# A table of expert units behind every image, and 28 expert chunks hosted inside the image steps

## The chip, the cores and the metric

The kernel runs on one core of a Trainium2 chip. The metric is the time of one execution on the device, in microseconds (us). The cores' engines work side by side, each on its own queue in order, and meet only at semaphores: TensorE (PE) multiplies, VectorE (DVE) and ScalarE (ACT) do the elementwise work and the reductions, GpSimd (POOL) issues the indirect transfers and one addition, SyncE (SP) issues the plain transfers.

## The reference

32 images of 224x224 are cut into 1024 patches each and pass through one attention block and one block of eight experts. Cut to what matters:

```python
h = patches @ W.T + b + pos                      # 32 images, 1024 tokens, 64 wide
q, k, v = h @ Wq.T + bq, h @ Wk.T + bk, h @ Wv.T + bv
prob = softmax(q @ k.T / 8)                      # 1024 x 1024 for each image
h = layernorm(h + (prob @ v) @ Wo.T + bo)
x = h.reshape(32 * 1024, 64)
idx = argmax(softmax(x @ gate_w + gate_b))       # one expert of 8 for each token
pos = cumsum(one_hot(idx)) at idx - 1            # the token's place in its expert
kept = pos < C                                   # C = ceil(1.25 * 32768 / 8) = 5120
y = relu(x @ w1[idx] + b1[idx]) @ w2[idx] + b2[idx]
h = layernorm(h + nan_to_num(y * prb * kept))
```

A token's expert and its place are known only when its own image and all before it have been through attention and gate.

## The kernel before

**Two kinds of work.** Attention goes image by image. The experts' part goes by *chunks* of 4 units; a *unit* is 256 rows of one expert, so that one weight set serves it. There are `NC` = 34 chunks. The gate gives every token a slot in the region of its expert in a table in HBM (`slots`), and POOL scatters an image's 1024 rows there (`scatter`, 8 indirect transfers). A chunk is loaded from `slots` by SP (`load_chunk`: rows into `b_in`, weights into `b_w`), goes through two matmul layers (`rows_turn`, `up`, `down`, `turn_back`) and a last layernorm on DVE and ACT, and POOL scatters its 1024 finished rows to the output (`spread_out`, 8 indirect transfers, 6 for the last chunk).

**Steps.** The program is written out in steps b = -2 to 33 (`run_windows`). In step b the scores, exponents and weighted sums of image b run, beside the row maxima of image b+1, the projection of b+2, the tail of image b-1 (`attend`, the residual, layernorm, gate) and the slots of image b-2 (`positions` on PE, `slot_read` and `slot_index` on DVE, `scatter` on POOL). Each engine's order within a step is fixed by hand: a loop over k or j = 0 to 7, one for each block of 128 keys or queries, with the other work hung in between.

**Chunks inside steps.** `HOST` says which steps host a chunk: chunk c runs in step `HOST[c]`, its last part on DVE in the two steps behind, and its `spread_out` two steps behind. Before, these are the steps 6 to 32, so chunks 0 to 26 (`INSIDE` = 27). The seven others run behind the last step, in `rounds` on every engine. In `rounds` the POOL queue holds nothing but `spread_out`; ahead of chunk `LAST` = 29, the first with rows of image 31, it waits until every earlier output transfer has landed.

**Tables.** Which unit a chunk takes is not known ahead. DVE writes it into `tab` by some dozen small instructions, each waiting for the one before: `count_rows` (1 instruction, in `slot_read`), `full_units` (4), `past_experts` (2), `name_units` (3), and afterwards `take_units` (3), which marks those units as taken. `IMAGE[c]` is the image behind whose slots the units of chunk c are named; an image in `TABLES` gets such a table, and PE then makes two more small matmuls in `positions`. Before, `TABLES` holds the even images 2 to 28, and 30 and 31: a table of an even image names 8 units, for the chunks of two steps.

**Where the table work stands on DVE.** In a normal step b, with image b-2 in `TABLES`: `take_units(b - 3)` and `full_units(b - 2)` at j = 1 ahead of `attend(b - 1)`, `past_experts` at j = 2 ahead of `weigh`, `name_units` at j = 3. Before, the last three stand in even steps, `take_units` in odd ones. Steps 31 and 32 are different (`late_step`): there is no row maximum left to do, the residual is added on DVE instead of POOL (`last_residual`), and on ACT `norm_root` comes right after exponent 2 of the step, ahead of exponent 3. Between `last_residual(30)` and `sum_squares(30)` DVE has `take_units(28)`.

**SP.** `load_chunk` for the chunk of step b+1 stands at the end of step b. It waits for `tab`, for the scatters of image `IMAGE[c]`, and its four weight loads wait for scores of step b.

Of the kernel before, what the change touches and what calls it, by code (L numbers as in the profile page):

```python
# [16 lines left out]
NB = 32  # L17
# [40 lines left out]
PACK = 1 << 19  # L58
NC = (NB * S // UNIT + E) // 4

HOST = [*range(6, NB + 1)]
INSIDE = len(HOST)


def image_of(c):

    if c < INSIDE:
        return (HOST[c] - 3) // 2 * 2
    for n in (NB - 4, NB - 2):
        if c < n - 1:  # L70
            return n
    return NB - 1


IMAGE = [image_of(c) for c in range(NC)]
# [12 lines left out]
def build(nc, x, posT, wqk, wide, deep, w, out):  # L88
    slots = nc.dram_tensor("slots", (SLOTS, ROW), F32, kind="Internal").ap()
    with ExitStack() as ctx:  # L90
# [141 lines left out]
        def per_token(ap, n):  # L232

            return ap.unsqueeze(2).broadcast_to([P, NT, n])

        def per_column_e(ap, n):

            return ap.unsqueeze(1).broadcast_to([P, n, E])
# [20 lines left out]
        def back_place(c):  # L259

            return p_misc[:, 1, :] if c < INSIDE and HOST[c] < NB else p_st[:, 1, :]

# [91 lines left out]
        def chunk_of(b):  # L354

            return HOST.index(b) if b in HOST else None

# [29 lines left out]
        def _(sp):  # L387
# [20 lines left out]
            def load_chunk(c):  # L408
# [21 lines left out]
                def weights_in():  # L430
                    if c >= NBUF:
                        sp.wait_ge(b_yT_ready, c - NBUF + 1)
                    for k in range(2 * PAIRS):
                        v, u = k // 2, k % 2
                        if c < INSIDE:

                            sp.wait_ge(st_done, NT * (HOST[c] - 1) + NT // 2 + 1 + k)
                        sp.dma_start(b_w[:, r, v, u, :], w[bass.ds(e[k], 1), :, :].rearrange("a k f -> (a k) f"))\
# [55 lines left out]
        def _(pe):  # L494
# [125 lines left out]
            def rows_turn(c):  # L620
# [4 lines left out]
                if c < INSIDE:  # L625
                    pe.wait_ge(t_ready, min(HOST[c], NB))
                elif c == INSIDE:
# [329 lines left out]
        def _(dve):  # L957
# [83 lines left out]
            def attend(n, p):  # L1041

                def step(i, ins):
                    ins.then_inc(tail_v, 1)
                    dve.wait_ge(tail_v, TS * n + i)

                dve.wait_ge(turn_done, n + 1)
                dve.wait_ge(v_ready, 2 * n + 2)
                after(dve, uc_ready, n)
                step(1, dve.reciprocal(rs[:, :].rearrange("p (a t) -> p a t", a=2), turned[:, :, :, GT - 1]))  # L1050
                step(2, dve.scalar_tensor_tensor(out=mk[:, :], in0=hh[:, p, :, GH - 1], scalar=0.0,
                                                 in1=rs[:, :], op0=ALU.not_equal, op1=ALU.mult))
                step(3, dve.scalar_tensor_tensor(out=rm[:, :], in0=hh[:, p, :, GH - 2], scalar=0.0,
                                                 in1=mk[:, :], op0=ALU.not_equal, op1=ALU.mult))
                dve.tensor_tensor(four(tt[:, :, :]), turned[:, :, :, 0:CG],  # L1055
                                  four(per_token(rm[:, :], CG)), ALU.mult).then_inc(t_ready, 1)

            def last_residual(n):

                dve.wait_ge(t_ready, n + 1)  # L1060
                dve.wait_ge(rows_ready, n)
                dve.wait_ge(sq_ready, n)
                dve.tensor_tensor(uc[:, :, :], tt[:, :, :], hh[:, n % 2, :, 0:CG], ALU.add)\
                    .then_inc(uc_ready, 1)
# [12 lines left out]
            def sum_squares(n):  # L1077
                dve.wait_ge(sq_ready, n + 1)
                after(dve, rstd_ready, n)
                dve.tensor_reduce(vs[:, :], sq[:, :, :], AX.X, ALU.add).then_inc(vs_ready, 1)  # L1080
# [40 lines left out]
            def table(ins):  # L1121

                steps[0] += 1
                ins.then_inc(table_step, 1)
                dve.wait_ge(table_step, steps[0])
# [5 lines left out]
            def full_units(n):  # L1131


                last = n == TABLES[-1]
                if last:
                    table(dve.tensor_scalar(t_up[:, :], t_cnt[:, :], float(UNIT - 1), None, ALU.add))
                ends = t_up if last else t_cnt
                table(dve.tensor_scalar(t_f[:, :], ends[:, :], -UNIT, None, ALU.bitwise_and))
                table(dve.tensor_tensor(t_av[:, :], t_f[:, :], c_next[:, 0:E], ALU.subtract))
                if last:  # L1140
                    table(dve.tensor_tensor(t_s[:, 0:E], t_cnt[:, :], t_av[:, :], ALU.subtract))
                table(dve.tensor_tensor(t_cum[:, :, :], per_column_e(t_av[:, :], E),
                                        c_tri[:, :].rearrange("p (a b) -> p a b", b=E), ALU.mult))
                table(dve.tensor_reduce(t_c[:, 1:E + 1], t_cum[:, :, :], AX.X, ALU.add))

            def past_experts(n):

                k = TAKEN[TABLES.index(n)]
                table(dve.tensor_tensor(t_ge[:, 0:k, :], c_unit[:, 0:k].unsqueeze(2).broadcast_to([P, k, E]),
                                        per_column_e(t_c[:, 1:E + 1], k), ALU.is_ge))  # L1150
                begin, end = (t_s, t_cnt) if n == TABLES[-1] else (c_next, t_f)
                table(dve.tensor_tensor(t_da[:, :], begin[:, 1:E + 1], end[:, :], ALU.subtract))

            def name_units(n):


                i = TABLES.index(n)
                k, at = TAKEN[i], STARTS[i]
                table(dve.scalar_tensor_tensor(out=t_rd[:, 0:k, :], in0=per_column_e(t_da[:, :], k), scalar=float(PACK),
                                               in1=t_ge[:, 0:k, :], op0=ALU.add, op1=ALU.mult))  # L1160
                table(dve.tensor_reduce(t_r[:, 0:k], t_rd[:, 0:k, :], AX.X, ALU.add))
                dve.scalar_tensor_tensor(out=tab[:, at:at + k], in0=t_r[:, 0:k], scalar=c_next[:, 0:1],
                                         in1=c_unit[:, 0:k], op0=ALU.add, op1=ALU.add).then_inc(table_ready, 1)
# [15 lines left out]
            def take_units(n):  # L1179

                rows_taken = float(UNIT * TAKEN[TABLES.index(n)])
                table(dve.tensor_scalar(t_m[:, :], t_c[:, :], rows_taken, None, ALU.min))
                table(dve.tensor_tensor(t_x[:, :], t_m[:, 1:E + 1], t_m[:, 0:E], ALU.subtract))
                table(dve.tensor_tensor(c_next[:, 0:E], c_next[:, 0:E], t_x[:, :], ALU.add))
# [23 lines left out]
            def weigh(c):  # L1208
                r = c % NBUF
                dve.wait_ge(b_back_done, c + 1)  # L1210
                if c >= 1:
                    dve.wait_ge(b_num_ready, c)
                dve.tensor_tensor(b_p[:, :, :].rearrange("p (u j) d -> p u j d", u=2), turned_back(c),
                                  b_in[:, r, :, :, D].unsqueeze(3).broadcast_to([P, 2, CT, D]), ALU.mult)\
                    .then_inc(b_p_ready, 1)

            def finite(c):

                dve.wait_ge(b_p_ready, c + 1)
                dve.tensor_scalar(b_fin[:, :, :], b_p[:, :, :], 0.0, 0.0, ALU.mult, ALU.is_equal)  # L1220
                dve.tensor_scalar(b_pos[:, :, :], b_p[:, :, :], 0.0, 1e4, ALU.max, ALU.min)
# [27 lines left out]
            def sum_of_squares(c):  # L1249
                dve.wait_ge(b_sq_ready, c + 1)  # L1250
                if c >= 1:
                    dve.wait_ge(b_sd_ready, c)
                dve.tensor_reduce(b_vs[:, :], b_sq[:, :, :], AX.X, ALU.add).then_inc(b_vs_ready, 1)

            def scaled(c):
                dve.wait_ge(b_rs_ready, c + 1)
                if c >= NOUT:
                    dve.wait_ge(b_scattered[c % NOUT], 16 * NT * (c // NOUT))
                dve.tensor_tensor(b_o[:, c % NOUT, :, :], b_c[:, :, :], per_token(b_rs[:, :], D), ALU.mult)\
                    .then_inc(b_o_ready, 1)  # L1260

            def late_step(n, q, back, done):

                last = n == NB - 1
                sum_of_squares(done)
                attend(n, q)
                last_residual(n)
                if not last:
                    take_units(n - 2)
                scaled(done)  # L1270
                sum_squares(n)
                weigh(back)
                gate_logits(n)
                gate_gaps(n)
                gate_choice(n)
                norm_rows(n)
                finite(back)
                slot_read(n)
                probability(n, q)
                slot_index(n, q)  # L1280
                to_numbers(back)
                residual_sum(back)
                centre(back)
                full_units(n)
                past_experts(n)
                if last:
                    name_last(n)
                else:
                    name_units(n)
                    take_units(n)  # L1290
# [224 lines left out]
```

## Time and profile before

| | us |
|---|---|
| median of 3 runs (1049.13 to 1049.90) | 1049.55 |
| the profiled execution | 1052.52 |
| its span, the time that the rows cover | 1050.7 |
| PE busy in the span | 945.6 (90%) |
| DVE busy | 854.0 (81%) |
| ACT busy | 708.1 (67%) |
| POOL busy | 586.2 (56%) |
| granted TensorE clock, mean share | 0.953 |

The profiled execution took 1.8 us more than its span, and 3.0 us more than the median of the unprofiled runs. In the page's 40 slices PE is at nine tenths or more from slice 3 to slice 34 and falls off in the last five; POOL is busiest there.

### The profile page before, as it was taken

How to read it: one execution, taken by the hardware profiler on the slowest of the kernel's cores; microseconds unless marked ns; L12 is line 12 of the kernel's file. 1: busy time of each engine (PE TensorE's matmuls, PEld its weight loads, DVE VectorE, ACT ScalarE, POOL GpSimd, SP SyncE). 2: the span in 40 equal slices, each digit the busy share in tenths (PEclk: the TensorE clock that was granted, in tenths of full speed). 3: DMA queues.
4: the chain of work that ended last, by engine and by line, in shares of the span. 5: the costliest groups of instructions: out<-in, count | busy, mean ns of one | idle time of the engine just before them, and what ended most of it. 6: DMA issues, size and time to landing. Idle time of an engine off the chain costs nothing.

```text
span 1050.7 us, 19710 instructions
## 1 busy us (share of the span) xinstructions
PE 945.6 (90%) x6046; PEld 530.5 (50%) x6046; DVE 854.0 (81%) x1771; ACT 708.1 (67%) x1254; POOL 586.2 (56%) x564
## 2 busy tenths in 40 slices
PE   4799999999999999999999999999999999846640
PEld 2355555555555555555555555555555555433320
DVE  3667788789898989999898989898999988675561
ACT  2365665777777777777777777777777766636650
POOL 0003333335666666666666666666666666776775
PEclk9699999999999999999999999999999999958775
DMA  3322223333434343343434333434333432235200
GB/s 96 80 64 68 59 60 100 99 92 88 117 83 119 96 106 93 98 107 103 110 95 109 105 103 84 118 89 113 102 99 91 108 96 71 87 86 175 63 20 11
DMA packets 72504, 96.25 MB, mean 92 GB/s; under 512 B 15923, under 2 KB 52230, under 8 KB 72398
## 3 DMA queue, kind: packets, MB, share of 16 engines
q1 hardware_dynamic: 55566, 77.87, 28.9%
q0 software_dynamic: 16832, 17.11, 5.1%
q8 instruction: 49, 0.80, 0.3%
q14 instruction: 57, 0.47, 0.1%
HBM read 43.68 MB, written 18.11 MB: 59 GB/s over the span
## 4 chain that ended last, share of the span: by engine, by line
PE 51%; DVE 29%; issue 9%; ACT 8%; DMA 1%; POOL 1%; SPq 0%; POOLq 0%; ACTq 0%; DVEq 0%
PE p_u L601 14%; PE p_st L579 9%; DVE mx L1028 8%; PE p_misc L616 6%; PE p_misc L547 4%; PE p_misc L664 3%; ACT uu L807 3%; PE p_sm L561 3%; PE p_st L583 3%; DVE lo L1020 2%; DVE qk L1013 2%; PE p_misc L524 2%; PE p_sm L680 2%; ACT b_h L852 2%; PE p_misc L680 1%
## 5 line engine op out<-in xcount | busy, mean ns | idle before, releaser
L1399 POOL DMA_INDIRECT slots<-rows,idx x256 | 251.2, 981 | 275.5 <-issue 166.9
L1412 POOL DMA_INDIRECT out<-b_o,b_ix x270 | 294.7, 1091 | 86.7 <-issue 81.7
L1028 DVE TENSOR_REDUCE mx<-p_sm 128x1 f32<-128x1024 f32 x252 | 306.9, 1218 | 35.1 <-PE p_sm L563 33.7
L802 ACT ACTIVATE pT<-p_st 128x1024 f32<-128x1024 f32 x256 | 262.0, 1023 | 92.2 <-PE p_st L585 80.8
L601 PE MATMUL p_u<-pT,vv 128*64 128x512 f32 x1024 | 254.1, 607 | 0.0
L579 PE MATMUL p_st<-hi,hx 64*128 64x512 f32 x256 | 127.4, 498 | 6.2 <-ACT pT L802 4.4
L581 PE MATMUL p_st<-hx,hi 64*128 64x512 f32 x256 | 127.4, 498 | 0.0
L601 PEld LDWEIGHTS p_u<-pT,vv 128*64 128x64 f32 x1024 | 61.8, 136 | 106.2 <-issue 94.4
L579 PEld LDWEIGHTS p_st<-hi,hx 64*128 64x128 f32 x256 | 47.0, 184 | 128.5 <-issue 100.3
L561 PE MATMUL p_sm<-kh,hi 64*128 64x512 f32 x252 | 100.7, 399 | 5.1 <-DMA hx<-hi 3.5
L852 ACT ACTIVATE b_h<-p_misc,b_w 128x256 f32<-128x256 f32 x244 | 95.8, 476 | 13.1 <-PE p_misc L664 6.5
L579 PE MATMUL p_st<-lo,hx 64*128 64x512 f32 x256 | 100.8, 394 | 0.0
L581 PE MATMUL p_st<-lx,hi 64*128 64x512 f32 x256 | 100.7, 394 | 0.0
L585 PE MATMUL p_st<-hx,lo 64*128 64x512 f32 x256 | 100.5, 393 | 0.0
L583 PE MATMUL p_st<-hi,lx 64*128 64x512 f32 x256 | 100.5, 393 | 0.0
L563 PE MATMUL p_sm<-kh,hx 64*128 64x512 f32 x252 | 100.5, 399 | 0.0
L1390 POOL TENSOR_TENSOR uc<-tt,hh 128x576 f32<-128x576 f32 x30 | 39.3, 1312 | 80.3 <-DVE tt L1055 80.3
L773 ACT ACTIVATE qk<-p_misc 128x1024 f32<-128x1024 f32 x32 | 32.9, 1027 | 72.7 <-PE p_misc L524 71.4
L547 PE MATMUL p_misc<-w_px,xt 114*128 114x137 f32 x504 | 76.7, 296 | 0.0
L547 PEld LDWEIGHTS p_misc<-w_px,xt 114*128 114x128 f32 x504 | 63.7, 192 | 23.1 <-issue 23.1
L664 PE MATMUL p_misc<-b_xT,b_w 64*128 64x256 f32 x488 | 68.6, 400 | 4.3 <-ACT b_xT L841 2.5
L616 PE MATMUL p_misc<-w_j,uu 128*128 128x73 f32 x512 | 64.2, 279 | 7.6 <-ACT uu L807 7.0
(189 smaller groups left out, 1818.7 us busy)
## 6 DMA issues: line engine op xcount, KB each, us to landing
b_w<-in_w SPq DMA_DIRECT2D x136, 193.5 KB
hx<-hi SPq DMA_DIRECT2D x64, 256.0 KB, 3.6
b_in<-slots SPq DMA_DIRECT2D x136, 66.0 KB
lx<-lo SPq DMA_DIRECT2D x32, 256.0 KB, 3.1
xt<-in_x SPq DMA_DIRECT2D x32, 196.0 KB
out<-b_o,b_ix POOLq DMA_INDIRECT x270
kh<-kh SPq DMA_DIRECT2D x32, 128.0 KB, 2.3
lx<-lo SPq DMA_DIRECT2D x32, 128.0 KB, 3.0
```

The costliest lines, as they stand in the source:

```text
L547: last = pe.matmul(projected(n, r)[:, j // 2, (j % 2) * GP:(j % 2 + 1) * GP], xt[0:KTOK, n % 3, t * P:(t + 1) * P], w_px[:, :], start=True ...
L561: pe.matmul(max_place(n, j)[:, 0, :], hi[t][0:D, j * P:(j + 1) * P], kh[n % 2][0:D, 0:HALF], start=True, stop=True)
L579: pe.matmul(p_st[:, 0, :], hx[t][0:D, kt], upper[t][0:D, 0:HALF], start=first, stop=False, skip_group_check=k > 0)
L581: pe.matmul(p_st[:, 1, :], hi[t][D:P, kt], lower[t][D:P, HALF:S], start=first, stop=False, skip_group_check=k > 0)
L583: pe.matmul(p_st[:, 0, :], lx[t][0:D, kt], hi[t][0:D, 0:HALF], start=False, stop=k > 0, skip_group_check=k > 0)
L601: last = pe.matmul(p_u[c:c + D, a, :], vv[:, p, NT - 1 - k, :], pT[k % 4][:, a * HALF:(a + 1) * HALF], start=(r == 0), stop=(r == 3))
L616: last = pe.matmul(p_misc[:, j // 4, (j % 4) * GT:(j % 4 + 1) * GT], uu[:, j * P:(j + 1) * P], w_j[:, :], start=True, stop=True)
L802: act.activation(pT[k % 4][:, :], flat(p_st), ACT.Exp).then_inc(exp_done, 1)
L852: act.activation(b_h[:, f, u, v, :], place[:, u, v * UNIT:(v + 1) * UNIT], ACT.Relu, bias=b_w[:, r, v, u, W1C + HB * D + f:W1C + HB * D + ...
L1028: dve.tensor_reduce(mx[:, p, at:at + 1], flat(max_place(n, j)), AX.X, ALU.max).then_inc(max_done, 1)
L1399: pool.indirect_dma_start(slots, bass.IndirectOffsetOnAxis(ap=idx[:, p, j:j + 1], axis=0), rows[:, p, j, :], None, bounds_check=SLOTS - 1, ...
L1412: pool.indirect_dma_start(out_rows, bass.IndirectOffsetOnAxis(ap=b_ix[:, o, j:j + 1], axis=0), b_o[:, o, j, :], None, bounds_check=T - 1, ...
```

## The change

`HOST` begins at step 5 instead of 6: 28 chunks run inside steps and six behind them. `image_of` names the units of the chunk in step b behind image b-3, for every b. `TABLES` becomes the images 2 to 31, 30 tables instead of 16, each of the first 28 with 4 units. Where an even step had 10 table instructions on DVE and an odd step 3, every step from 5 on has 13; altogether 14 tables of 13 instructions more. `late_step(30)` gets the table of image 29 in four new lines.

```diff
--- before.py
+++ after.py
@@ -58,18 +58,15 @@
 PACK = 1 << 19
 NC = (NB * S // UNIT + E) // 4
 
-HOST = [*range(6, NB + 1)]
+HOST = [*range(5, NB + 1)]
 INSIDE = len(HOST)
 
 
 def image_of(c):
 
     if c < INSIDE:
-        return (HOST[c] - 3) // 2 * 2
-    for n in (NB - 4, NB - 2):
-        if c < n - 1:
-            return n
-    return NB - 1
+        return HOST[c] - 3
+    return NB - 2 if c < NB - 3 else NB - 1
 
 
 IMAGE = [image_of(c) for c in range(NC)]
@@ -1267,6 +1264,10 @@
                 last_residual(n)
                 if not last:
                     take_units(n - 2)
+                    full_units(n - 1)
+                    past_experts(n - 1)
+                    name_units(n - 1)
+                    take_units(n - 1)
                 scaled(done)
                 sum_squares(n)
                 weigh(back)
```

`NC`, `LAST`, the buffers and the work of a chunk are the same. Line numbers in the changed kernel are 3 lower than before up to `late_step`, and 1 higher behind it.

**DVE in step 31**, between the last residual (`uc`) and the sum of squares (`vs`) of image 30. `t_m`, `t_x` and `c_wide` are `take_units`, `t_f` to `t_c` `full_units`, `t_ge` and `t_da` `past_experts`, `t_rd` to `tab` `name_units`; `b_o` is the end of a hosted chunk. Before:

```order
L1063 TENSOR_TENSOR uc<-tt,hh 128x576
L1182 TENSOR_SCALAR t_m<-t_c 128x9
L1183 TENSOR_TENSOR t_x<-t_m 128x8
L1184 TENSOR_TENSOR c_wide<-c_wide,t_x 128x8
L1259 TENSOR_TENSOR b_o<-b_c,b_rs 128x512
L1080 TENSOR_REDUCE vs<-sq 128x8
```

Changed, the last 12 of the 17 rows from `uc` to `vs` (ahead of these stand `uc`, the same three `take_units` rows, `t_f` and `t_av`):

```order
L1139 TENSOR_TENSOR t_cum<-t_av,c_wide 128x64
L1141 TENSOR_REDUCE t_c<-t_cum 128x8
L1146 TENSOR_TENSOR t_ge<-c_wide,t_c 128x32
L1149 TENSOR_TENSOR t_da<-c_wide,t_f 128x8
L1156 SCALAR_TENSOR_TENSOR t_rd<-t_da,t_ge 128x32
L1158 TENSOR_REDUCE t_r<-t_rd 128x4
L1159 SCALAR_TENSOR_TENSOR tab<-t_r,c_wide 128x4
L1179 TENSOR_SCALAR t_m<-t_c 128x9
L1180 TENSOR_TENSOR t_x<-t_m 128x8
L1181 TENSOR_TENSOR c_wide<-c_wide,t_x 128x8
L1256 TENSOR_TENSOR b_o<-b_c,b_rs 128x512
L1077 TENSOR_REDUCE vs<-sq 128x8
```

Twelve small instructions have come in between `uc` and `vs`.

**DVE in step 11**, an odd step that hosts a chunk, from the row maximum (`mx`) of j = 1 on; `rs` to `tt` are `attend`, `b_p` is `weigh`. Before:

```order
L1028 TENSOR_REDUCE mx<-p_sm 128x1
L1182 TENSOR_SCALAR t_m<-t_c 128x9
L1183 TENSOR_TENSOR t_x<-t_m 128x8
L1184 TENSOR_TENSOR c_wide<-c_wide,t_x 128x8
L1050 RECIPROCAL rs<-p_misc 128x8
L1051 SCALAR_TENSOR_TENSOR mk<-hh,rs 128x8
L1053 SCALAR_TENSOR_TENSOR rm<-hh,mk 128x8
L1055 TENSOR_TENSOR tt<-p_misc,rm 128x576
L1028 TENSOR_REDUCE mx<-p_sm 128x1
L1213 TENSOR_TENSOR b_p<-p_misc,b_in 128x512
L1259 TENSOR_TENSOR b_o<-b_c,b_rs 128x512
```

Changed:

```order
L1025 TENSOR_REDUCE mx<-p_sm 128x1
L1179 TENSOR_SCALAR t_m<-t_c 128x9
L1180 TENSOR_TENSOR t_x<-t_m 128x8
L1181 TENSOR_TENSOR c_wide<-c_wide,t_x 128x8
L1135 TENSOR_SCALAR t_f<-t_cnt 128x8
L1136 TENSOR_TENSOR t_av<-t_f,c_wide 128x8
L1139 TENSOR_TENSOR t_cum<-t_av,c_wide 128x64
L1141 TENSOR_REDUCE t_c<-t_cum 128x8
L1047 RECIPROCAL rs<-p_misc 128x8
L1048 SCALAR_TENSOR_TENSOR mk<-hh,rs 128x8
L1050 SCALAR_TENSOR_TENSOR rm<-hh,mk 128x8
L1052 TENSOR_TENSOR tt<-p_misc,rm 128x576
```

Four rows of a table (`t_f` to `t_c`) stand ahead of `attend`; behind the next `mx` come `t_ge` and `t_da` ahead of `b_p`, and three more behind the `mx` after that. An even step gets the three rows `t_m` to `c_wide` instead.

**POOL from step 31 to the end**: `slots` are the scatters of the images 29, 30 and 31, `out` the finished rows of chunks. Before:

```order
L1399 DMA slots<-rows,idx 264448x66 x8
L1412 DMA out<-b_o,b_ix 32768x64 x8
L1399 DMA slots<-rows,idx 264448x66 x8
L1412 DMA out<-b_o,b_ix 32768x64 x8
L1399 DMA slots<-rows,idx 264448x66 x8
L1412 DMA out<-b_o,b_ix 32768x64 x70
```

Changed:

```order
L1400 DMA slots<-rows,idx 264448x66 x8
L1413 DMA out<-b_o,b_ix 32768x64 x8
L1400 DMA slots<-rows,idx 264448x66 x8
L1413 DMA out<-b_o,b_ix 32768x64 x8
L1400 DMA slots<-rows,idx 264448x66 x8
L1413 DMA out<-b_o,b_ix 32768x64 x62
```

Behind the last scatter stand 62 output transfers instead of 70, those of one chunk fewer.

## Rows read from the trace of the kernel before

**Rows 1.** Page: the chain of work that ended last, shares by engine.
```profile
PE 51%; DVE 29%; issue 9%; ACT 8%; DMA 1%; POOL 1%; SPq 0%; POOLq 0%; ACTq 0%; DVEq 0%
```

**Rows 2.** Timeline, PE: start, length, then the transpose that opens steps 5, 6, 10, 11, 12.
```profile
158.82 0.33 PE L568 MATMUL p_sm<-c_wide,mx 128*128 128x128 f32 x1
182.67 0.33 PE L568 MATMUL p_sm<-c_wide,mx 128*128 128x128 f32 x1
...
295.43 0.33 PE L568 MATMUL p_sm<-c_wide,mx 128*128 128x128 f32 x1
323.70 0.33 PE L568 MATMUL p_sm<-c_wide,mx 128*128 128x128 f32 x1
351.92 0.33 PE L568 MATMUL p_sm<-c_wide,mx 128*128 128x128 f32 x1
```

**Rows 3.** Timeline, DVE in step 10: its only idle times (in brackets, with releaser).
```profile
304.57 0.21 DVE L1050 RECIPROCAL rs<-p_misc 128x8 f32<-128x8 f32 x1 [0.28 <-PE p_misc L616]
...
308.58 0.69 DVE L1213 TENSOR_TENSOR b_p<-p_misc,b_in 128x512 f32<-128x512 f32 x1 [0.86 <-PE p_misc L641]
```

**Rows 4.** Timeline, DVE: a comparison of step 4's table; below, POOL's addition.
```profile
146.47 1.77 DVE L1149 TENSOR_TENSOR t_ge<-c_wide,t_c 128x32 f32<-128x32 f32 x1
...
146.84 1.34 POOL L1390 TENSOR_TENSOR uc<-tt,hh 128x576 f32<-128x576 f32 x1
```

**Rows 5.** Timeline, DVE in step 31: `take_units(28)`, then table 30 from first to last.
```profile
897.39 0.26 DVE L1182 TENSOR_SCALAR t_m<-t_c 128x9 f32<-128x9 f32 x1
...
897.88 0.17 DVE L1184 TENSOR_TENSOR c_wide<-c_wide,t_x 128x8 f32<-128x8 f32 x1
898.08 0.69 DVE L1259 TENSOR_TENSOR b_o<-b_c,b_rs 128x512 f32<-128x512 f32 x1
...
909.88 0.17 DVE L1138 TENSOR_SCALAR t_f<-t_cnt 128x8 uint32<-128x8 uint32 x1
...
912.31 0.17 DVE L1184 TENSOR_TENSOR c_wide<-c_wide,t_x 128x8 f32<-128x8 f32 x1
```

**Rows 6.** Timeline, ACT and PE in step 31: who waits for `vs`, and on.
```profile
899.40 0.30 ACT L819 ACTIVATE sd<-vs,b_eps 128x8 f32<-128x8 f32 x1 [1.28 <-DVE vs L1080]
...
901.40 0.50 PE L579 MATMUL p_st<-hi,hx 64*128 64x512 f32 x1 [1.54 <-ACT pT L802]
```

**Rows 7.** Stretches: length, busy PE, PEld, DVE, ACT, POOL, clock, DMA share, GB/s.
```profile
900.70:904.10 3.40, 2.70 (x30) 1.82 (x30) 2.90 (x12) 2.49 (x6) 2.79 (x3) 1.00 0.21 54
...
917.70:921.10 3.40, 1.82 (x17) 1.70 (x17) 2.06 (x6) 0.05 (x1) 2.66 (x3) 1.00 0.34 112
921.10:934.70 13.60, 8.87 (x48) 4.81 (x46) 9.36 (x30) 4.91 (x13) 10.56 (x11) 0.50 0.40 116
...
951.90:955.20 3.30, 3.30 (x16) 1.52 (x14) 0.00 (x0) 0.27 (x1) 2.69 (x3) 0.50 0.88 254
```

**Rows 8.** Timeline, PE: the 16 matmuls of one `down` at either clock.
```profile
910.35 1.95 PE L680 MATMUL p_misc<-b_h,b_w 128*64 128x256 f32 x16
...
951.74 3.60 PE L680 MATMUL p_sm<-b_h,b_w 128*64 128x256 f32 x16 [0.78 <-ACT b_h L852]
```

**Rows 9.** Timeline, POOL behind the steps: first transfer of chunks 27, 28, 29; the last.
```profile
969.10 1.11 POOL L1412 DMA_INDIRECT out<-b_o,b_ix  x1 [2.89 <-DVE b_o L1259]
...
979.94 1.48 POOL L1412 DMA_INDIRECT out<-b_o,b_ix  x1 [0.30 <-issue]
...
992.63 1.19 POOL L1412 DMA_INDIRECT out<-b_o,b_ix  x1 [2.12 <-issue]
...
1042.39 0.97 POOL L1412 DMA_INDIRECT out<-b_o,b_ix  x1 [0.30 <-issue]
```

**Rows 10.** Timeline, SP loads chunk 29's rows; ACT copies chunk 28's; page: time to landing.
```profile
946.59 2.07 SPq L428 DMA_DIRECT2D b_in<-slots  x4
...
949.61 0.61 ACT L834 ACTIVATE b_x<-b_in 128x512 f32<-128x512 f32 x1
...
kh<-kh SPq DMA_DIRECT2D x32, 128.0 KB, 2.3
```

## The prediction

> **What bounds the kernel now.** I read the shares of the chain that ended last first [rows 1]: PE carries 51% and DVE 29%, so the kernel is bound by PE with DVE close behind, and a change that loads DVE to relieve the end has to be costed at both. Next I read the step length off PE's own timeline, from the transpose that opens each step [rows 2]. Step 5, the last without a chunk, took 182.67 - 158.82 = 23.85 us. In the steady state, with a chunk, an even step (10) took 28.27 and an odd one (11) 28.22, although DVE has 10 table instructions in the one and 3 in the other. Then the idle times of DVE inside step 10 [rows 3]: 0.28 us before `rs` and 0.86 before `b_p`, both waits for PE, 1.14 us together and no others. DVE is nearly full there, but PE sets the pace. Last I read the two places where this is not so. In step 31 ACT stands 1.28 us until DVE's `vs` is there, and PE stands 1.54 until ACT's exponent [rows 6], so the path runs through DVE. Behind the steps POOL has one idle time of 2.89 us, where it waits for the finished rows of chunk 27, and one of 2.12 ahead of chunk 29; from there to the start of its last transfer, 49.76 us later, it issues without a stop [rows 9]. That end is POOL's, and its beginning hangs on the compute chain of the first chunk behind the steps.
>
> **The change, part by part.**
>
> *One chunk fewer behind the steps.* Between POOL's wait for the first chunk behind and its wait ahead of chunk 29 there were two chunks (27, 28), now there is one (28). The removed one is 979.94 - 969.10 = **10.8 us** [rows 9]. Both waits stay, and chunk 29 and its followers are what they were. So the gain is 10.8 us only if the first chunk's rows are ready no later than now, measured from the end of the steps.
>
> *Step 5 hosts a chunk.* It goes from 23.85 to the length of a hosting step with a table, 28.27: **+4.4 us**. The end of that chunk falls into steps 6 and 7, which then hold what the steady steps hold.
>
> *Thirteen table instructions in every step.* An even step gets `take_units`, three instructions. From `t_m` to `c_wide` and the next start they take 898.08 - 897.39 = 0.69 us [rows 5]. The first 0.28 of it falls into the wait before `rs`, the rest moves `attend` by 0.4 and is taken up by the 0.86 before `b_p` [rows 3], behind which nothing has changed. I take 0, since 0.69 is less than 1.14. The cover is the two waits for PE; without it the price would be up to 0.4 us a step. An odd step becomes what an even one is, which costs the measured difference, 28.27 - 28.22 = 0.05 us, in 12 steps (7 to 29): **+0.6 us**. This includes the two small matmuls of `positions` on PE.
>
> *POOL's addition beside the tables.* In step 4 `t_ge` took 1.77 us, where it lay over POOL's addition of 1.34 [rows 4]. [...] The steady steps with a table already include whatever `t_ge` loses to that addition, and they are 0.05 longer than those without; both start behind `tt`, so they move together. I take nothing beyond the 0.05. Steps 5 to 7 may show one or two long ones (0 to 1 us).
>
> *The table of image 29 in step 31.* It comes between `uc` and `vs` of image 30, 12 instructions in a row, each waiting for the last. The same 12 for image 30 took from 909.88 to 912.31, and the last of a `take_units` holds the next for 0.20 (897.88 to 898.08): 2.43 + 0.20 = **2.6 us** [rows 5]. Nothing hides them. ACT already waits for `vs`, and behind `norm_root` in its queue stand exponent 3 and all exponents after it; PE's scores 4 wait for exponent 3 [rows 6]. So PE's wait grows from 1.54 to 4.2 us. Later in the step DVE has slack, and the rest moves along with PE.
>
> *TensorE's clock in step 31.* [...] The price is bounded by 0 (the low clock lies inside the wait) and by several stretches. The shortest, 951.90 to 955.20, cost 3.60 - 1.95 = 1.65 us on the 16 matmuls of `down` [rows 8]. I take one such stretch: **+1.6 us**; the upper bound is two, +3.3. [...]
>
> *Loads.* SP's wait for the scatter of image b-2 was there in even steps, which load for odd ones, and now is in odd steps too. Behind it in the queue stand only the weight loads, which wait for the end of the step, and the next step's transfers. I take 0. At the end, chunk 29 is the second behind the steps instead of the third. Its rows were issued until 946.59 + 2.07 = 948.66; the nearest landing time is 2.3 us for a 64 to 128 KB transfer, which gives 951.0, and ACT wanted the rows of the chunk in that place at 949.61 [rows 10]. That would be 1.4 us late at most. POOL's scatters move less than the compute chain (POOL does not run through step 31's wait), so part of it is made good: bounds 0 and 1.4, I take **+0.5**.
>
> *Sum* against the profiled execution's span: -10.8 + 4.4 + 0.6 + 2.6 + 1.6 + 0.5 = **-1.1 us**, 1050.7 to 1049.6. The execution around it took 1.8 us more than its span and 3.0 more than the median of the unprofiled runs. I carry the difference over to that median: 1049.55 - 1.1 = **1048.4 us**.
>
> **The rivals.**
>
> *A. The clock holds in step 31,* or falls only inside the wait. For it: the stretch 900.70 to 904.10, with the end of the wait of 1.54 us in it, ran at 1.00 [rows 6, 7]. Against it: 4.2 us. Time: 1049.55 - 2.7 = 1046.8.
>
> *B. Step 31's table is hidden.* For it: nothing but that PE has other short waits behind it. Against it: both waits in the rows name this very chain. Without the 2.6 and the 1.6 the sum is -5.3: 1044.2.
>
> *C. DVE becomes the bound of the hosting steps,* which makes the kernel slower. `attend` is later by 0.69 - 0.28 = 0.4 us in each, and if PE waits for `tt` or for the row maximum behind it, the two turns of `rows_turn` and `turn_back` are late by as much. It decides from the point where the three extra instructions and anything they collide with cost more than DVE's 1.14 us of idle time. Price: 0.4 x 25 steps = 10 us, 1048.4 + 10 = 1058. Against it: an odd step takes 7 more instructions at the price of 0.05 us.
>
> *D. The end is held up by more:* the clock stays low for two stretches (+1.6 more), or chunk 29's rows are late by the whole 1.4 us and a late start makes a low stretch fall on the path of chunk 28. Some 1.6 to 3 us more: 1050 to 1051.5, around 1050.8.
>
> That the change doesn't do what it says can be left out: the queues show both the 62 transfers and the tables.
>
> **How the numbers follow.** The forecast has a chance of 0.40 (own range 1047.3 to 1049.6), A 0.25, B 0.07, C 0.08, D 0.20. A measurement of this kernel can tell about 0.2% from no change, here 2.1 us, so "same" is 1047.45 to 1051.65. Faster than that: a good quarter of the forecast (0.11), four fifths of A (0.20), B (0.07): 0.38. Slower: C and a third of D, 0.15. Same: the rest, 0.47. The range leaves out C, B and the two ends of the others: 1045.6 to 1051.6.
>
> **What would show it.** In the profile of the changed kernel: step 5 at 28.2 us and all steps to 29 at 28.3 (with C 28.6 or more, and no idle time of DVE before `b_p`); `vs` in step 31 later behind `uc` by 2.6 us, and PE's wait behind it at 4.2 us; a granted clock of 0.50 within 4 us of that wait (with A none until image 31's tail); POOL's first wait behind the steps ahead of chunk 28 and its last transfer 10.8 us earlier after the shift of the steps. The prediction is wrong if step 31 is not longer by 2.6 us or more, if steady steps differ from 28.3 by over 0.1, or if the stretch from the end of step 32 to the end shrinks by clearly less than 10 us.

## The result and the profile after

| | before | after |
|---|---|---|
| median of 8 runs of each, made beside each other (us) | 1049.59 (1049.13 to 1050.97) | 1052.49 (1051.85 to 1053.27) |
| the profiled execution (us) | 1052.52 | 1053.14 |
| its span (us) | 1050.7 | 1051.3 |

The changed kernel is slower: 2.9 us by the medians, ratio 1.002 with an interval of 1.0011 to 1.003. The prediction was 1048.4 us, 1.1 us faster, with a range up to 1051.6. The result lies outside it.

Page of the changed kernel: busy times by engine, then the chain that ended last, the lines that answer to [rows 1].

```profile
PE 946.8 (90%) x6074; PEld 531.1 (51%) x6074; DVE 879.5 (84%) x1953; ACT 708.5 (67%) x1254; POOL 578.6 (55%) x564
...
DVE 43%; PE 37%; issue 9%; ACT 7%; POOL 2%; DMA 1%; SPq 0%; POOLq 0%; DVEq 0%; ACTq 0%
```

The first thing to see is the chain. PE's share fell from 51% to 37% and DVE's rose from 29% to 43%. PE is as busy as before (945.6 and 946.8 us), so hardly anything was added there; more of the chain now runs through DVE.

Timeline of the changed kernel, PE: the transposes that open the steps 5, 6, 12, 13 and 31, then in step 31 the wait for the exponent and the turn of image 31's sums.

```profile
156.96 0.33 PE L565 MATMUL p_sm<-c_wide,mx 128*128 128x128 f32 x1
185.18 0.33 PE L565 MATMUL p_sm<-c_wide,mx 128*128 128x128 f32 x1
...
355.26 0.33 PE L565 MATMUL p_sm<-c_wide,mx 128*128 128x128 f32 x1
383.67 0.33 PE L565 MATMUL p_sm<-c_wide,mx 128*128 128x128 f32 x1
...
895.11 0.33 PE L565 MATMUL p_sm<-c_wide,mx 128*128 128x128 f32 x1
...
911.23 0.79 PE L576 MATMUL p_st<-hi,hx 64*128 64x512 f32 x1 [4.08 <-ACT pT L799]
...
929.05 2.01 PE L613 MATMUL p_misc<-w_j,uu 128*128 128x73 f32 x16 [1.12 <-ACT uu L804]
```

The same two points of step 31 in the kernel before.

```profile
887.83 0.33 PE L568 MATMUL p_sm<-c_wide,mx 128*128 128x128 f32 x1
...
916.86 2.01 PE L616 MATMUL p_misc<-w_j,uu 128*128 128x73 f32 x16 [1.12 <-ACT uu L807]
```

Timeline of the changed kernel, POOL: the first transfers of the chunks 28 and 29, and the last transfer, the lines that answer to [rows 9].

```profile
982.02 1.12 POOL L1413 DMA_INDIRECT out<-b_o,b_ix  x1 [4.14 <-DVE b_o L1256]
...
994.59 1.37 POOL L1413 DMA_INDIRECT out<-b_o,b_ix  x1 [2.13 <-issue]
...
1043.68 0.97 POOL L1413 DMA_INDIRECT out<-b_o,b_ix  x1 [0.30 <-issue]
```

With these rows the two profiled spans fall into pieces that can be set beside the sum of the prediction:

| piece | before | after | difference | predicted |
|---|---|---|---|---|
| start to step 5 | 158.82 | 156.96 | -1.9 | 0 |
| step 5 | 23.85 | 28.22 | +4.4 | +4.4 |
| steps 6 to 30 | 705.16 | 709.93 | **+4.8** | +0.6 |
| step 31's start to POOL's wait for the first chunk behind | 81.27 | 86.91 | +5.6 | +4.7 |
| from there to the wait ahead of chunk 29 | 23.53 | 12.57 | -11.0 | -10.8 |
| from there to the last transfer | 49.76 | 49.09 | -0.7 | 0 |
| last transfer to the end | 8.31 | 7.62 | -0.7 | 0 |

Two things stand out. The steady steps cost 4.8 us where 0.6 was expected; a step takes 383.67 - 355.26 = 28.41 us instead of 28.25 (mean of an even and an odd one, [rows 2]). And the first piece is hardly the change's: up to step 5 nothing was to be expected of it, and TensorE's granted clock ran differently. Both executions had reached 1.00 in the stretch ahead of this one; in this one it was back at 0.51 before and stayed at 1.00 after. First before, then after (length, busy times, granted clock, DMA share, GB/s):

```profile
47.30:50.70 3.40, 3.40 (x12) 1.70 (x14) 1.59 (x2) 1.92 (x2) 0.00 (x0) 0.51 0.58 119
```

```profile
47.30:50.70 3.40, 3.40 (x22) 1.43 (x20) 1.55 (x2) 1.51 (x2) 0.00 (x0) 1.00 0.58 134
```

The profiled execution of before reached step 5 at 158.82; the changed kernel and the seven experiments reached it at 156.2 to 157.5, but for one at 159.0 (dose_before_wait), the only other one whose clock was near a half (0.52) in this stretch. Without that piece the spans differ by 0.6 + 1.9 = 2.5 us, near the 2.9 between the medians. Whoever compares the two spans alone sees 0.6 us and looks for an error of 1.7; the error is 4.

### The profile page after: what moved, and what is told of

Same layout as the page of the kernel before. It is cut to its first block, busy times and chain, and to the rows that moved or that the text cites. A ratio compares the mean times of both kernels' runs of the same rounds, so it can differ in the third digit from the quotient of the medians.

```text
span 1051.3 us, 19952 instructions
## 1 busy us (share of the span) xinstructions
PE 946.8 (90%) x6074; PEld 531.1 (51%) x6074; DVE 879.5 (84%) x1953; ACT 708.5 (67%) x1254; POOL 578.6 (55%) x564
## 4 chain that ended last, share of the span: by engine, by line
DVE 43%; PE 37%; issue 9%; ACT 7%; POOL 2%; DMA 1%; SPq 0%; POOLq 0%; DVEq 0%; ACTq 0%
DVE mx L1025 13%; PE p_u L598 10%; PE p_misc L613 6%; PE p_st L576 5%; ACT uu L804 3%; DVE lo L1017 3%; DVE qk L1010 3%; PE p_misc L544 2%; PE p_sm L677 2%; PE p_sm L558 2%; PE p_misc L521 2%; DVE b_n L1228 2%; PE p_st L580 2%; DVE vs L1077 2%; DVE b_n L1226 2%
## 5 line engine op out<-in xcount | busy, mean ns | idle before, releaser
L1413 POOL DMA_INDIRECT out<-b_o,b_ix x270 | 285.8, 1059 | 91.9 <-issue 82.3
```

Of the source, the lines that this page charges most:

```text
L1413: pool.indirect_dma_start(out_rows, bass.IndirectOffsetOnAxis(ap=b_ix[:, o, j:j + 1], axis=0), b_o[:, o, j, :], None, bounds_check=T - 1, ...
```

## Where the steady steps lose: the rows

Timeline of the changed kernel, DVE: first `b_p` of step 12, the key step `qk` in step 13 and the next `b_p`; last, `vs` of step 31.

```profile
368.56 0.69 DVE L1210 TENSOR_TENSOR b_p<-p_misc,b_in 128x512 f32<-128x512 f32 x1 [0.61 <-PE p_misc L638]
...
387.62 1.09 DVE L1010 TENSOR_TENSOR qk<-qk,p_misc 64x896 f32<-64x896 f32 x1
...
396.99 0.69 DVE L1210 TENSOR_TENSOR b_p<-p_misc,b_in 128x512 f32<-128x512 f32 x1 [0.62 <-PE p_misc L638]
...
908.52 0.68 DVE L1077 TENSOR_REDUCE vs<-sq 128x8 f32<-128x512 f32 x1
```

DVE still waits some 0.6 us ahead of `b_p` in every steady step (0.61 in step 12). By rival C's own sign ("no idle time of DVE before `b_p`") DVE is not the bound; by the chain it is. The chain of work that ended last, changed kernel, steps 12 to 13, shows how both can be true (start, length, what):

```profile
387.62 1.10 DVE qk L1010
388.77 0.62 issue
...
389.79 1.04 ACT uu L804
...
390.87 2.01 PE p_misc L613 x16
...
396.46 0.45 PE p_misc L638 x4
...
396.99 0.06 DVE b_p L1210
```

This is a loop. DVE's key step `qk` releases ACT (the keys' high part, then the sums `uu` in ACT's queue), ACT releases PE's turn of the sums, PE's queue goes on to `turn_back`, which releases `b_p`. Behind `b_p` the rows show no idle time of DVE until the next step's `qk`: the rest of the step, then `lo`, `sh`, `count_rows`, the slots. Every instruction between `b_p` and `qk` delays the next `b_p`, however long the wait ahead of it is. That wait is the part of the loop in which PE works; it covers only what stands between `qk` and `b_p`.

The kernel before has the same loop, shown by its DVE rows of the steps 11 and 12 (that of step 10 is in [rows 3]).

```profile
327.43 1.09 DVE L1013 TENSOR_TENSOR qk<-qk,p_misc 64x896 f32<-64x896 f32 x1
...
336.73 0.69 DVE L1213 TENSOR_TENSOR b_p<-p_misc,b_in 128x512 f32<-128x512 f32 x1 [1.43 <-PE p_misc L641]
...
355.72 1.09 DVE L1013 TENSOR_TENSOR qk<-qk,p_misc 64x896 f32<-64x896 f32 x1
...
365.08 0.69 DVE L1213 TENSOR_TENSOR b_p<-p_misc,b_in 128x512 f32<-128x512 f32 x1 [0.88 <-PE p_misc L641]
```

From `b_p` to the start of `qk` it took 18.85 us behind an even step's `b_p` (308.58 to 327.43, with `name_units` in it, 0.65 us) and 18.99 behind an odd one's (with `count_rows`, 0.2 us, and without `name_units`). In the odd loop one instruction of the chunk's `finite` (`b_pos`) took 0.67 us instead of 0.41, and DVE was held up for some 0.3 us more between its instructions. One such place is the layernorm's `rstd` of ACT, here in the chain of before (start, length, what):

```profile
347.19 0.22 ACT rstd L821
```

It ends at 347.41, and DVE's next instruction starts at 347.43; ahead of it the chain runs through ACT and PE back to 336.69. So in the odd loop PE set the pace, and DVE had a little slack behind `b_p` too. The changed kernel has `name_units` and `count_rows` in every loop, 368.56 to 387.62, 19.06 us, near the 18.85 of the even loop plus the 0.2 of `count_rows`. The whole loop, from one `b_p` to the next, took 28.15 and 28.35 before, 28.25 in the mean, and now 28.43 (368.56 to 396.99). The excess, 0.18 us in some 25 steps, is 4.5 us, about the size of the error.

## The experiments

Each kernel differs from the changed one by the edit shown and was timed beside the kernel before. Differences from the changed kernel are taken through the two ratios to before.

### tables_alone: the tables without the 28th chunk

```diff
-HOST = [*range(5, NB + 1)]
+HOST = [*range(6, NB + 1)]
```

> The changed kernel with HOST back at steps 6 to 32 (27 chunks inside, seven behind) and still a table of 4 units behind every image: the tables alone. Theory (loop): in a hosting step DVE runs without a stop from b_p to the key steps (qk) of the next step, and through ACT and PE this closes a loop that a table lengthens; so every step with a table costs 28.42 to 28.45 us, against 28.25 on average before, and step 31 is 4.9 us longer. Expected against before: 23 x 0.19 + 4.9 = +9.3 us. Rival (the prediction's sum): 12 x 0.05 + 2.6 + 1.6 = +4.8 us, steps at 28.27.

Measured: 1059.46 us beside 1050.79, ratio 1.0085 (1.0069 to 1.0102), +8.9 us, near the 9.3 of the loop and well above the 4.8 of the prediction's sum. Two openers of steady steps on PE's timeline:

```profile
351.82 0.33 PE L565 MATMUL p_sm<-c_wide,mx 128*128 128x128 f32 x1
380.28 0.33 PE L565 MATMUL p_sm<-c_wide,mx 128*128 128x128 f32 x1
```

28.46 us, although nothing is hosted in step 5. So the price of the steady steps belongs to the tables, and the hosting alone is worth what is left: 1.002 against 1.0085, about 6.8 us by the ratios and 5.8 by the medians, where the prediction's two terms give 10.8 - 4.4 = 6.4. That half of the change is sized right.

### dose_before_wait and dose_behind_wait: the same 0.6 us on either side of DVE's wait

Both add three small DVE instructions to every hosting step, into a tile that nobody reads. In one they stand at j = 1, ahead of `attend`, and so between `qk` and `b_p`; in the other at j = 3, behind `name_units`, and so between `b_p` and `qk`. The comments in the diff below say which run has which call; the declaration of the tile is left out.

```diff
+            def idle_steps():
+                for _ in range(3):
+                    table(dve.tensor_scalar(t_idle[:, :], c_base[:, :], 1.0, None, ALU.mult))
...
+                    if j == 1 and chunk_of(b) is not None:     # dose_before_wait
+                        idle_steps()
...
+                    if j == 3 and chunk_of(b) is not None:     # dose_behind_wait
+                        idle_steps()
```

> The changed kernel with three more small DVE instructions (a chain of three on an unused tile, 0.6 us in all, the result is not used) in every step with a chunk, at j = 1 ahead of attend, so ahead of DVE's idle time before b_p (0.55 us). Theory (loop, the place decides): the idle time takes them up, steps stay within 0.1 us of 28.44, 0 to +3 us in all against the changed kernel. Rival (the amount decides): +0.6 x 26 = +16 us.

> The same three instructions in every step with a chunk, at j = 3 behind name_units, so behind the idle time before b_p, in DVE's stretch without a stop up to the next step's key steps. Theory (loop): each step is longer by the whole 0.6 us, 29.0 to 29.1, +14 to +16 us against the changed kernel. Rival (PE sets the step, DVE's chain only looks critical): under +5 us.

Timeline of dose_before_wait, PE (two step openers) and DVE (the three instructions, the next `b_p`):

```profile
357.63 0.33 PE L566 MATMUL p_sm<-c_wide,mx 128*128 128x128 f32 x1
386.02 0.33 PE L566 MATMUL p_sm<-c_wide,mx 128*128 128x128 f32 x1
```

```profile
367.25 0.58 DVE L1127 TENSOR_SCALAR t_idle<-c_wide 128x8 f32<-128x8 f32 x3
...
370.95 0.69 DVE L1215 TENSOR_TENSOR b_p<-p_misc,b_in 128x512 f32<-128x512 f32 x1
```

The same of dose_behind_wait:

```profile
358.81 0.33 PE L566 MATMUL p_sm<-c_wide,mx 128*128 128x128 f32 x1
387.81 0.33 PE L566 MATMUL p_sm<-c_wide,mx 128*128 128x128 f32 x1
```

```profile
372.28 0.69 DVE L1215 TENSOR_TENSOR b_p<-p_misc,b_in 128x512 f32<-128x512 f32 x1 [0.62 <-PE p_misc L639]
```

Ahead of the wait the dose ate the idle time before `b_p`, all 0.6 us of it, and the step stayed at 28.39 us; the kernel took 1.003 (1.0017 to 1.0042) of before, which can't be told from the changed kernel's 1.002. Behind the wait the same dose made the step 29.00 us, longer by 0.59, all of it, and the wait ahead of `b_p` is still there, 0.62 us. The kernel took 1.0172 (1.0155 to 1.0189), by the ratios some 16 us more than the changed one. In the two profiled executions the difference is 14.6 us, all of it in the steps 5 to 30 (752.79 against 738.15), some 0.6 us in each step from 7 on; the steps 5 and 6 hardly grew. This pair settles it. The same instructions on the same engine are free or cost their full length, and the idle time that stands in the row says nothing of those behind it.

### names_early: `name_units` moved to the other side of the wait

```diff
                         if j == 2:
                             past_experts(b - 2)
+                            name_units(b - 2)
                     if back is not None and j == 2:
                         weigh(back)
-                    if b - 2 in TABLES[:-1]:
-                        if j == 3:
-                            name_units(b - 2)
```

> The changed kernel with name_units moved from j = 3 (behind b_p and the row maximum of j = 3) to j = 2, right behind past_experts and ahead of b_p. The same instructions. Theory (loop): 0.57 us leave the stretch from b_p to qk and go into DVE's idle time of 0.55 ahead of b_p; PE then bounds the steps, 28.1 to 28.25 instead of 28.44, over 25 steps -5 to -8 us against the changed kernel, so -2 to -5 us against before. Rival (the amount of work on DVE sets the step, wherever it stands): no change against the changed kernel, +2.9 us against before.

Timelines of names_early, PE (two step openers) and DVE (the last of `name_units`, then `b_p`), and its chain's shares:

```profile
355.55 0.33 PE L565 MATMUL p_sm<-c_wide,mx 128*128 128x128 f32 x1
383.83 0.33 PE L565 MATMUL p_sm<-c_wide,mx 128*128 128x128 f32 x1
```

```profile
368.57 0.22 DVE L1159 SCALAR_TENSOR_TENSOR tab<-t_r,c_wide 128x4 uint32<-128x4 f32 x1
368.71 0.68 DVE L1210 TENSOR_TENSOR b_p<-p_misc,b_in 128x512 f32<-128x512 f32 x1
```

```profile
PE 57%; DVE 22%; issue 9%; ACT 8%; POOL 2%; DMA 1%; SPq 0%; POOLq 0%; ACTq 0%; DVEq 0%
```

The step is 28.28 us, the idle time ahead of `b_p` is used up, and the chain is PE's again. The time is 1051.43 us, ratio 1.0001 (0.9991 to 1.0011), some 2 us less than the changed kernel. The theory named the place rightly and the gain too high: it put 5 to 8 us on it, with PE bounding the steps at 28.1 to 28.25, so 0.2 to 0.3 us off each. Only some 0.13 came off: with the loop shorter PE became the bound at 28.28, hardly above the 28.25 of before. As in the odd loop of before, its chain passes behind `b_p` from PE to ACT's `rstd` (it ends at 379.32) and then to DVE (379.34). Steps 5 to 30 took 2.9 us less than in the changed kernel (735.24 against 738.15).

### late_off: step 31's table out of the path

```diff
                     take_units(n - 2)
-                    full_units(n - 1)
-                    past_experts(n - 1)
-                    name_units(n - 1)
-                    take_units(n - 1)
                 scaled(done)
...
                 finite(back)
+                if not last:
+                    full_units(n - 1)
+                    past_experts(n - 1)
+                    name_units(n - 1)
+                    take_units(n - 1)
                 slot_read(n)
```

> The changed kernel with the table of image 29 in step 31 moved from between uc and vs to behind finite, ahead of slot_read: off the path uc, vs, norm_root, exponent 3. Theory: PE's wait falls from 4.08 to 1.5 us and the granted clock stays at 1.00 in step 31, so the step is 2.6 + 2.3 = 4.9 us shorter; -4.9 us against the changed kernel, -2 against before. Rival (the clock falls in any case, or the compute chain behind makes it good): -2.6 us or less.

Timeline of late_off, PE: step 31's opener, the wait for the exponent, the turn of image 31's sums; below, the stretch behind the wait.

```profile
895.36 0.33 PE L565 MATMUL p_sm<-c_wide,mx 128*128 128x128 f32 x1
...
908.78 0.50 PE L576 MATMUL p_st<-hi,hx 64*128 64x512 f32 x1 [1.39 <-ACT pT L799]
...
924.23 2.01 PE L613 MATMUL p_misc<-w_j,uu 128*128 128x73 f32 x16 [1.12 <-ACT uu L804]
```

```profile
908.00:918.00 10.00, 8.10 (x63) 4.43 (x65) 9.07 (x37) 7.02 (x14) 7.56 (x9) 1.00 0.16 43
```

The wait is 1.39 us instead of 4.08, the clock holds, and the turn comes 28.87 us behind the opener instead of 33.94: 5.1 us, as expected. The time is 1050.04 us, ratio 0.9992 (0.9982 to 1.0002), only some 3 us less than the changed kernel. The expectation of 4.9 us for the whole was too high. In the profiled executions 0.7 us is given back between the turn and the end of POOL's wait for chunk 28, which comes 4.4 us earlier behind step 31's opener (82.50 us). Another 1.15 us goes between there and the end, 0.98 of it in POOL's last 38 transfers, those of the chunks 29 to 33: from the start of the first to the start of the last they took 50.07 us here and 49.09 in the changed kernel. In the nine profiles, with the same 38 transfers in each, that stretch took 47.97 (both) to 50.07, and 49.76 before. What makes it vary isn't shown; a profiled difference of 1 us there is not the edit's.

### clock_held: the wait kept, the clock kept up

PE gets 14 matmuls with an unread result behind scores 3, where the wait begins. They hold no one up: DVE's chain to `vs` is as long as in the changed kernel (13.41 us behind the opener).

```diff
                         scores(b, k)
+                    if b == NB - 1 and k == 3:
+                        for _ in range(14):
+                            pe.matmul(p_sm[:, 0, :], hi[b % 3][0:D, 0:P], kh[b % 2][0:D, 0:HALF],
+                                      start=True, stop=True)
```

> The changed kernel with 14 extra matmuls (512 columns, into an unused bank, the result is not read) on PE in step 31 behind scores 3, so inside the wait of 4.08 us for exponent 3. Theory: the granted clock stays at 1.00 through step 31, the wait for vs is as long as in the changed kernel, and the turn of image 31's sums starts 31.5 us behind the step's start instead of 33.9: -2.4 us against the changed kernel. Rival (what lies behind vs is late for another reason than the clock): no change.

Timeline of clock_held, PE: step 31's opener, the 14 matmuls, the turn of image 31's sums; below, the stretch in which the changed kernel has the low clock.

```profile
893.93 0.33 PE L565 MATMUL p_sm<-c_wide,mx 128*128 128x128 f32 x1
...
905.80 3.34 PE L715 MATMUL p_sm<-kh,hi 64*128 64x512 f32 x14
...
925.50 2.01 PE L613 MATMUL p_misc<-w_j,uu 128*128 128x73 f32 x16 [1.12 <-ACT uu L808]
```

```profile
909.20:916.00 6.80, 5.95 (x48) 3.24 (x48) 5.99 (x24) 5.18 (x11) 5.28 (x6) 1.00 0.41 111
```

And the changed kernel at the same place (the wait, then the low clock):

```profile
906.30:909.70 3.40, 0.85 (x6) 0.36 (x6) 3.16 (x11) 0.43 (x3) 2.54 (x3) 1.00 0.07 20
909.70:916.50 6.80, 5.27 (x30) 2.97 (x30) 4.45 (x20) 4.22 (x9) 5.23 (x6) 0.50 0.34 95
```

The clock stayed at 1.00 and the turn came 31.57 us behind the opener instead of 33.94. So the low clock costs 2.4 us and the table 2.5, and together they are the 4.9 us by which step 31 grew to that point (from 29.03). The whole time, ratio 1.0009 (0.9998 to 1.002), is some 1.2 us below the changed kernel, with intervals that overlap; the 2.4 is read from the trace, the gain of the whole is not shown by the times alone. The granted clock was 0.50 behind 4.08 us of waiting, 1.00 with the wait filled (0.90 us of it was left), and 1.00 with late_off's wait of 1.39.

### both: names_early and late_off together

> The changed kernel with both moves: name_units ahead of b_p, and step 31's table of image 29 behind finite. If the two causes are apart and add up: -10 to -13 us against the changed kernel, -7 to -10 against before, about 1040 to 1043. If the end (POOL) swallows one of them: no better than the better one of the two alone.

Timeline of both, PE: two step openers.

```profile
355.57 0.33 PE L565 MATMUL p_sm<-c_wide,mx 128*128 128x128 f32 x1
383.87 0.33 PE L565 MATMUL p_sm<-c_wide,mx 128*128 128x128 f32 x1
```

1046.69 us beside 1050.79, ratio 0.996 (0.9946 to 0.9974): 4.2 us faster than before, and some 6 us faster than the changed kernel. It beats both. That is about half of the 10 to 13 us expected against the changed kernel: names_early and late_off each bring less than expected, for the reasons given there. The two repairs about add up (2 and 3 us alone, some 6 together), and the result is near what the prediction's terms give without the costs of step 31: -10.8 + 4.4 + 0.6 + 0.5 = -5.3.

## Why the prediction was wrong

**The step that failed** is the price of "Thirteen table instructions in every step": 0 for an even step, since "0.69 is less than 1.14" and "The cover is the two waits for PE", and 0.05 us for an odd one, +0.6 us in all. It measured +4.8, because DVE's work behind the wait lies on a loop through ACT and PE that no wait in the rows covers. Both waits stand ahead of `b_p`. They cover `take_units`, `full_units` and `past_experts`, which stand ahead of them too: dose_before_wait shows that 0.6 us more there would still have been free. They don't cover `name_units` at j = 3 and `count_rows` in the next step, which stand behind them, and dose_behind_wait shows that there the whole 0.6 us is paid. The prediction's sentence "behind which nothing has changed" is true of an even step looked at alone: the three instructions of `take_units` are all that it gained. But `count_rows` was gained by the loop that ends in the next, odd step.

**The price from the step lengths** (0.05 us a step, +0.6) misread an alternating pattern. An even step with 10 table instructions took 28.27 and an odd one with 3 took 28.22, and from that the prediction took the price of a table. But each loop of before held one of the two groups, `name_units` or `count_rows`, never both and never none, so neither step was a measurement of a kernel without them. What one loop lost the next made up (28.15 and 28.35), and over the two PE kept the pace. With both groups in every loop DVE's way round takes 28.43, and the steps became as long. The steps also meet, by a hair, the prediction's own sign of being wrong, "if steady steps differ from 28.3 by over 0.1": 28.41 in step 12.

**Rival C** had the right kind of mechanism with the wrong place and price: it looked for DVE's idle time used up and 0.4 us a step. DVE kept its idle time, and the step grew by less than 0.2.

**Right:** the chunk fewer behind the steps (-10.8, measured -11.0); step 5 (+4.4, measured +4.4); the table in step 31 (+2.6: `vs` came 13.41 us behind the opener instead of 10.86) with PE's wait at 4.08 us against the 4.2 predicted; that the clock would fall there, as it had in [rows 7] behind a stretch in which PE was busy for about half the time. Here it was busy for 0.85 us of the 3.40 ahead of the low clock (906.30 to 909.70).

**Mis-sized:** the clock, +1.6 against 2.4. The prediction priced it by one short stretch, 1.65 us at the end of the kernel [rows 8]; here the low clock lasted 6.8 us and fell on the work of the step. The late rows of chunk 29, seen on ACT's timeline of the changed kernel with the wait for `vs`:

```profile
909.23 0.30 ACT L816 ACTIVATE sd<-vs,b_eps 128x8 f32<-128x8 f32 x1 [3.87 <-DVE vs L1077]
...
962.77 0.63 ACT L831 ACTIVATE b_x<-b_in 128x512 f32<-128x512 f32 x1 [1.06 <-DMA b_in<-slots]
```

1.06 us, inside the bounds of 0 and 1.4. From the turn of image 31's sums to POOL's wait the changed kernel took 52.97 us and before 52.24, so 0.7 us of the end is lost on this stretch, against the 0.5 taken; that it is these rows and nothing else was not tested. The last two pieces of the table above, 0.7 us better each where nothing was forecast, happen to outweigh it. The first of them lies within the spread given at late_off. That is luck, not a reading that was right.

**POOL's addition beside the tables** was rightly put at little. The durations of `t_ge` (L1146) in the changed kernel, minimum, median and maximum in ns:

```profile
L1146 DVE TENSOR_TENSOR t_ge<-c_wide,t_c x30: 193/394/1789, 144.6 to 949.9; 128x32 f32<-128x32 f32 x29, 128x160 f32<-128x160 f32 x1
```

The median is 0.39 us, and where POOL makes no addition, in step 31, `t_ge` takes 0.19. 24 of the 30 stand beside the last 0.33 to 0.35 us of an addition, as in step 12 (366.39 to 367.70 and 367.35 to 367.75), and take 0.39 to 0.40; the first three stand beside more of one and take 1.79, 1.31 and 0.65 us. So most take 0.2 us more, not the 1.6 more of the one in [rows 4]. That one starts 0.37 us ahead of POOL's addition and ends 0.06 us behind it (148.24 and 148.18), and each of the 27 here ends 0.04 to 0.07 us behind its addition, while the addition is no longer for it: 1.34 us in [rows 4], 1.30 to 1.34 in all 30 here. What holds `t_ge` up was not tested.

**The sum.** By the table of pieces, without the start: the steady steps were 4.2 us worse than their term and step 31 with what follows it 0.9 (most of it the clock), and the three last pieces together 1.5 better. -1.1 + 4.2 + 0.9 - 1.5 = +2.5, against +2.9 between the medians.

## What to carry to other kernels

The idle time that an in-order engine shows ahead of a wait is slack only for what stands between two points in its own queue: the instruction that sets off the other engines' work, and the wait for the result of that work. Here these are `qk` and `b_p`: with 0.6 us more work between them a step took 28.39 us, with the same work outside 29.00. So before an added instruction is called hidden, follow the loop: who releases the wait, who released that, and whether the path comes back to this engine with the new instruction in it. And where a pattern alternates, take the period over the whole pattern and list what each loop holds; the difference between its two halves is no price for either. Where a cost does lie on the loop, moving it to the other side of the wait can be enough: here some 2 us for one moved line, and 6 us with a table moved in step 31.

## What the runs showed of the hardware

One wait of 4.08 us on PE was followed by 6.8 us at half the clock, which cost 2.4 us of the path; 14 small matmuls, 3.34 us at the start of the wait, kept the clock at 1.00. A wait of 1.39 us at the same place left it at 1.00 too.

With the same start-up, the granted clock in the stretch 47.30 to 50.70 was 0.51 and 0.52 in two of the nine profiled executions and 1.00 in the seven others. Those two came to step 5 last, at 158.8 and 159.0, the others between 156.2 and 157.5. Whether the clock alone makes that difference was not tested. A profiled span of this kernel is therefore no measure for differences of 2 us; lengths between openers are.
